# Maxima rows sent from ScalarE's queue, SyncE's order and VectorE's statistics rearranged in a ViT tower

## The chip, the cores and the metric

The kernel runs on one core of one Trainium2 chip. The metric is the time of one execution on the device in microseconds, as the median of several runs. Engines are named as the profile names them: PE is TensorE's matmuls and PEld its weight loads, DVE is VectorE, ACT ScalarE, POOL GpSimd, SP SyncE; SPq and ACTq are rows of DMA instructions issued by SP and ACT.

## What is computed

32 images of 3 x 256 x 256 pass an edge filter, one attention block and one feed-forward block. Cut to what matters:

```
gray = 0.2989*R + 0.587*G + 0.114*B
h    = (|scharr_x(gray)| + |scharr_y(gray)|) / 2        # 256 rows of 256 = 256 tokens
h    = concat([cls_tok, h], axis=1)                     # 257 tokens
# attention, 16 heads of 16, causal
q, k, v = split(layernorm(h) @ w_qkv + b_qkv)
h    = h + softmax(mask(q @ k.T / 4)) @ v @ w_out + b_out
# feed-forward with fake quantisation: one scale for the whole tensor
xq   = fake_quant(layernorm(h), clip_x)                 # scale from max |layernorm(h)| over all images
h    = h + fake_quant(silu(xq @ Wg.T) * (xq @ Wu.T), clip_down) @ Wd.T
```

The scale of the feed-forward input needs the maximum over all images, so the kernel has two parts: attention for all images, then the feed-forward block.

## The kernel before

**Pipeline.** The attention part is a software pipeline. `pipeline(eng, step)` runs `step(n, n % 2)` for n from 0 to B + LAST - 1 on every engine: steps 0 to 7 are written out, 8 to 29 are a hardware loop of two steps per round, 30 and up are written out again. In step n the engines work on several images at once: image n is loaded and turned gray, bW = n - 1 is saved to and gathered from DRAM, bC = n - 2 goes through the edge convolution and the first layernorm, bP = n - 3 through the projections to queries, keys and values, bS = n - 4 through the scores, bT = n - 5 through the rest of the transposed scores, the exponentials and the outputs, and bO = n - 6 through the division by the softmax sum, the output projection, the residual and the statistics of the second layernorm. The order within a step is written out by hand for each engine; semaphores do the rest, and a waiting instruction holds all that stands behind it on its engine.

**The two passes over the scores.** PE computes the scores of two heads at a time, `scores(u)` for u = 0..7 (L1005, mask added at L1008). DVE takes their row maxima, `maxima(bS, u)` (L788, L790). After u = 3 and u = 7 PE transposes the negated maxima of eight heads, `turn_max(half_)` (L1112), and DVE copies them into `mpart[half_]`, `split` (L805). A DMA puts them into rows SR and SR + 1 of `qst` (`max_rows`, L357), where they are two more rows of the contraction. So `scores_t(b, par, u)` (L1022), the scores transposed, come out with the maximum subtracted, and ACT takes their exponential (L580). `scores_t` waits for `m_loaded[0]` at u = 0 and for `m_loaded[1]` at u = 4. POOL masks the diagonal of two pairs of heads, `select(b, g)` (L463, L465), and `outputs(b, par, g)` (L1041) waits for that. In PE's order `scores_t(bS, par, 0)` stands ahead of `outputs(bT, odd, 3)`; in the next step `edges(0)` (L1060) waits for `msplit` of the second half, because both use the PSUM tile `M[1]`.

**SP, in order within a step.** The second half of the maxima of bT (`max_rows(bT, odd, 1)`); the moves of `yun` (L368, four DMAs) and `rec` (L372) for bO; gray planes of bW to DRAM (two DMAs); the next image (L304, three DMAs); the gathers of bW from DRAM (six DMAs, L393), behind waits for the gray planes saved and for the convolution of bC; the first half of the maxima of bS (`max_rows(bS, par, 0)`); the row of values of bS (L398); the keys (L404, six DMAs, waiting for the last `scores_t` of bT and `k_low`); the queries (L408, six DMAs, waiting for POOL's `q_low`); the softmax sums of bT (L412, `den`, four DMAs).

**ACT, in the middle of a step.** The exponential 7 of bT, the cast of `qpart` (L638), the exponential 0 of bS, the normalised rows `xhat` (L646), and so on; at the step's end the exponential 2 of bS and the scaling of image n by the gray weights (L660), then exponential 3 in the next step.

**DVE, around the block that is moved.** In step n: `split(bT, 1)`, `maxima(bS, 0)`, the reciprocal of `den` for bO (L862), `maxima(bS, 1)` to `(5)` with the edge work between them, the residual add of bO (L889), `maxima(bS, 6)`, `resid_stats(bO)` (L842 to L852), the values of bP, `maxima(bS, 7)`, then x2, its largest value and the mean for bO (L909 to L915). POOL's `pow` for bO (L507) lies between the two. At n = NW2 (36) DVE also prepares the weights of the down projection.

Of the kernel before, what the change touches and what calls it, by code (L numbers as in the profile page):

```python
# [10 lines left out]
P = 128  # L11
# [62 lines left out]
def vit_tower(nc, x, cls_tok, scharr, w_qkv, b_qkv, w_out, b_out, clip_x, clip_down,  # L74
# [8 lines left out]
    with ctx:  # L83
# [171 lines left out]
        LAST = 6  # L255
# [37 lines left out]
        NW0, NW2 = 3, B + LAST - 2  # L293
# [4 lines left out]
        def _(sp):  # L298
            xv = x.rearrange("b c (t p) w -> b p c t w", p=P)

            def load_x(b, par):
                src = xv[b] if isinstance(b, int) else xv[bass.ds(b, 1)].rearrange("o p c t w -> (o p) c t w")
                for c in range(CH):
                    sp.dma_start(xin[par][:, c, :, :], src[:, c]).then_inc(x_loaded[par], 16)  # L304
# [40 lines left out]
            def load_down():  # L345

                sp.wait_ge(gray_step, 2 * (B - 1))
# [5 lines left out]
            def max_rows(b, par, half_):  # L353

                if valid(b):
                    wait(sp, msplit, b, 2, half_ + 1)
                    sp.dma_start(qst[par][SR:SR + 2, 8 * half_:8 * half_ + 8, :], mpart[half_][:, :]  # L357
                                 ).then_inc(m_loaded[half_], 16)

            def step(n, par):  # L360
# [3 lines left out]
                max_rows(bT, odd, 1)  # L364
                if valid(bO):
# [6 lines left out]
                    sp.dma_start(rec[:, :], den[:, :]).then_inc(rec_moved, 16)  # L372
                if valid(bW):
                    wait(sp, gray_step, bW, 2, 2)
                    wait(sp, gst_loaded, bC - 1, 96, 96)
                    for t in range(QT):
                        sp.dma_start(gray_dram[odd][1 + P * t:1 + P * t + P, 1:1 + IMG],
                                     gray[:, t, :]).then_inc(gray_saved, 16)
# [5 lines left out]
                if valid(bW):  # L384
                    wait(sp, gray_saved, bW, 32, 32)
# [8 lines left out]
                max_rows(bS, par, 0)  # L394
# [23 lines left out]
                if isinstance(n, int) and n == B:  # L418
                    load_down()
# [4 lines left out]
        def _(pool):  # L424
# [43 lines left out]
            def step(n, par):  # L468
                bC, bP, bS, bT, bO = n - 2, n - 3, n - 4, n - 5, n - 6

                select(bT, 1)
                if valid(bS):
# [31 lines left out]
                if valid(bO):  # L504
                    wait(pool, ln2, bO, LN, LN)
                    wait(pool, x2_step, bO - 1, XS, XS)
                    nc.gpsimd.tensor_tensor(rstd2[:, rows2(bO)], ve2[:, :], half[:, :], ALU.pow  # L507
                                            ).then_inc(rs2_done, 1)
# [1231 lines left out]
```

## Time and profile before

| | |
|---|---|
| runs | 1157.46, 1163.3, 1168.16 us, median 1163.3 |
| the profiled execution | 1157.32 us, span 1155.6 us |
| mean granted clock of TensorE | 0.955 |
| busy share of the span | PE 86%, DVE 71%, ACT 59%, POOL 47% |

The span runs from the first to the last instruction of the one execution that was profiled. The attention part ends at about 936 us, the rest is the feed-forward block. Busy time does not count instructions that issue DMAs or handle semaphores. Times in the rows are microseconds from the start of the span.

### The profile page before, as it was taken

How to read it: one execution, taken by the hardware profiler on the slowest of the kernel's cores; microseconds unless marked ns; L12 is line 12 of the kernel's file. 1: busy time of each engine (PE TensorE's matmuls, PEld its weight loads, DVE VectorE, ACT ScalarE, POOL GpSimd, SP SyncE). 2: the span in 40 equal slices, each digit the busy share in tenths (PEclk: the TensorE clock that was granted, in tenths of full speed). 3: DMA queues.
4: the chain of work that ended last, by engine and by line, in shares of the span. 5: the costliest groups of instructions: out<-in, count | busy, mean ns of one | idle time of the engine just before them, and what ended most of it. 6: DMA issues, size and time to landing. Idle time of an engine off the chain costs nothing. (4 is left out here: it accounts for less than half of the span.)

```text
span 1155.6 us, 28368 instructions
## 1 busy us (share of the span) xinstructions
PE 989.1 (86%) x9742; PEld 709.7 (61%) x9742; DVE 814.8 (71%) x1969; ACT 686.6 (59%) x1171; POOL 538.1 (47%) x685
## 2 busy tenths in 40 slices
PE   6768989899999999899999998999888888887665
PEld 5446766666667676667676676676676643333454
DVE  4565566766677777766777777666666449998787
ACT  1345555666666566666666666665553237876776
POOL 5335455565555655565556555655443242220000
PEclk7888999999999999999999999999998989998989
DMA  7665555555556555555565555453422005501874
GB/s 200 149 138 145 132 136 143 133 128 134 133 154 151 137 148 148 129 130 138 152 152 135 149 148 130 130 139 100 116 63 63 12 1 200 200 1 50 265 227 151
DMA packets 156017, 152.93 MB, mean 132 GB/s; under 512 B 28175, under 2 KB 152372, under 8 KB 153908
## 3 DMA queue, kind: packets, MB, share of 16 engines
q1 hardware_dynamic: 154440, 152.14, 48.7%
q8 instruction: 35, 0.57, 0.2%
q10 hardware_dynamic: 1516, 0.01, 0.1%
q14 instruction: 26, 0.21, 0.1%
HBM read 67.49 MB, written 28.35 MB: 83 GB/s over the span
## 5 line engine op out<-in xcount | busy, mean ns | idle before, releaser
L580 ACT ACTIVATE prob<-ST 128x772 f32<-128x772 f32 x256 | 209.5, 818 | 152.4 <-PE ST L1022 147.7
L788 DVE TENSOR_REDUCE mneg<-SX 128x2 f32<-128x258 f32 x256 | 107.5, 420 | 224.7 <-PE SX L1008 224.5
L1005 PE MATMUL SX<-kst,qst 96*128 96x257 bf16 (+1 forms) x1024 | 160.4, 250 | 18.3 <-DMA qst<-qpart 7.6
L790 DVE TENSOR_REDUCE mneg<-SX 128x2 f32<-128x514 f32 x256 | 173.9, 679 | 0.0
L1022 PE MATMUL ST<-qst,kst 98*128 98x256 bf16 (+2 forms) x1536 | 138.0, 222 | 16.3 <-DMA qst<-mpart 15.9
L465 POOL TENSOR_SCALAR_AFFINE_SELECT prob<-prob 128x1016 f32<-128x1016 f32 x128 | 142.6, 1114 | 0.0
L1008 PE MATMUL SX<-mask_s,ident_b 128*128 128x256 bf16 x512 | 142.4, 278 | 0.0
L1022 PEld LDWEIGHTS ST<-qst,kst 98*128 98x128 bf16 x1536 | 120.3, 99 | 34.5 <-DMA qst<-mpart 14.7
L1005 PEld LDWEIGHTS SX<-kst,qst 96*128 96x128 bf16 x1024 | 91.9, 99 | 64.3 <-issue 28.4
L1041 PE MATMUL G<-prob,vaug 128*32 128x256 f32 (+2 forms) x3072 | 116.2, 280 | 11.9 <-POOL prob L465 10.6
L1041 PEld LDWEIGHTS G<-prob,vaug 128*32 128x32 f32 x3072 | 82.7, 111 | 44.6 <-POOL prob L465 16.0
L513 POOL TENSOR_TENSOR gray<-xin 128x512 f32<-128x512 f32 x32 | 40.6, 1269 | 93.9 <-ACT xin L660 93.8
L485 POOL TENSOR_TENSOR kpart<-kqr,kpart 128x512 bf16<-128x512 f32 x32 | 37.1, 1158 | 95.7 <-ACT kpart L632 95.7
L1060 PE MATMUL M<-gst,cw 102*32 102x256 f32 x1024 | 72.7, 401 | 9.0 <-DVE mpart L805 7.8
L1450 ACT ACTIVATE work<-GU,gsc 128x512 f32<-128x512 f32 x96 | 65.5, 686 | 23.6 <-PE GU L1658 23.3
L480 POOL TENSOR_TENSOR kqr<-kqr,kpart 128x512 f32<-128x512 f32 x32 | 37.0, 1157 | 88.9 <-ACT kqr L592 88.9
L463 POOL TENSOR_TENSOR tick<-half 128x2 f32<-128x2 f32 x128 | 30.1, 235 | 100.1 <-ACT prob L580 100.0
L1073 PE MATMUL M<-xT,wqkv 128*128 128x256 f32 x256 | 75.9, 421 | 0.0
L1711 PE MATMUL GU<-wdT,hq 128*128 128x256 bf16 x384 | 52.9, 304 | 25.8 <-ACT hq L1478 25.8
L1658 PE MATMUL GU<-work,wgT 128*128 128x512 bf16 x192 | 57.8, 383 | 18.1 <-ACT work L1436 11.0
L1084 PE MATMUL M<-xT,wqkv 128*128 128x256 f32 x256 | 72.3, 404 | 0.1
L1133 PE MATMUL M<-wop,yn 128*128 128x256 f32 x256 | 65.9, 402 | 0.8 <-DVE yn L870 0.8
(232 smaller groups left out, 2056.9 us busy)
## 6 DMA issues: line engine op xcount, KB each, us to landing
kst<-kpart SPq DMA_DIRECT2D x192, 128.5 KB, 2.5
xin<-in_x SPq DMA_DIRECT2D x96, 256.0 KB, 4.1
gst<-gray_dram SPq DMA_DIRECT2D x96, 256.0 KB
qst<-qpart SPq DMA_DIRECT2D x192, 128.0 KB, 2.4
h_dram<-hb SPq DMA_DIRECT2D x8, 1280.0 KB, 4.6
gray_dram<-gray SPq DMA_DIRECT2D x64, 128.0 KB, 3.0
result<-oy SPq DMA_DIRECT2D x32, 256.0 KB, 3.6
hb<-h_dram SPq DMA_DIRECT2D x5, 1280.0 KB, 6.6
```

Source lines behind the costliest of these rows:

```text
L465: nc.gpsimd.affine_select(p, p, [[0, 4], [-1, 2], [1, P - 1]], ALU.is_ge, 0.0, base=1, channel_multiplier=-1).then_inc(sel_done, 1)
L580: nc.scalar.activation(prob[:, g % 2, 2 * (u % 2):2 * (u % 2) + 2, 0:QEND], ST[:, :, 0:QEND], ACT.Exp).then_inc(exp_done, 1)
L788: nc.vector.tensor_reduce(mneg[:, 0, u // 4, 0, at], SX[:, :, S0:S0 + P + 1], AX.X, ALU.max, negate=True)
L790: nc.vector.tensor_reduce(mneg[:, 1, u // 4, 0, at], SX[:, :, S1:S1 + T], AX.X, ALU.max, negate=True).then_inc(max_done, 1)
L1005: mm(SX[:, r, at:at + k], qst[par][0:SR, 2 * u + r, P * t:P * t + P], kst[par][0:SR, 2 * u + r, 0:k], start=t == 1, stop=False)
L1008: last = mm(o, ident_b[:, :], mask_s[:, :, :], start=False, stop=True)
L1022: last = mm(ST[0:KEYS[k], r, QAT[k]:QAT[k] + QN[k]], kst[par_][:, i, KFIRST[k]:KFIRST[k] + KEYS[k]], qst[par_][:, i, Q0[k]:IMG], start=Tru ...
L1041: last = mm(o, vaug[par_][0:KEYS[k], k, head_at(4 * g + j), :], prob[0:KEYS[k], g % 2, j, QAT[k]:QAT[k] + QN[k]], start=k == 0, stop=k == ...
L1060: last = mm(M[1][32 * j:32 * j + 32, IMG * f:IMG * f + IMG], cw[:, f, :], gst[:, 4 * t + j, :], start=True, stop=True)
L1073: last = mm(M[m][:, 0:IMG], wqkv[:, c, D + P * m:D + P * m + P], xT[:, c, 1:T], start=c == 0, stop=c == KC - 1)
L1084: last = mm(M[0][:, 0:IMG], wqkv[:, c, P * m:P * m + P], xT[:, c, 1:T], start=c == 0, stop=c == KC - 1)
L1133: last = mm(M[0][:, D * t:D * t + D], yn[:, c, P * t:P * t + P], wop[:, c, :], start=c == 0, stop=c == KC - 1)
```

## The change

1. `LAST` goes from 6 to 7: one more step. A new index bR = n - 7 takes over the second layernorm: `resid_stats` comes one step later, between `maxima(bS, 0)` and `maxima(bS, 1)`, and the normalisation, its maximum and the mean between `maxima(bS, 1)` and `maxima(bS, 2)`. POOL's `pow` moves with it, to the place behind `select(bT, 1)`.
2. Both halves of the maxima are sent by ACT: `send_max(0)` behind the cast of `qpart` and ahead of exponential 0 of bS, `send_max(1)` behind the scaling of image n, at the step's end. SP's two `max_rows` are gone, so the value row and the keys follow the gathers directly.
3. The image is loaded by one DMA instead of three, the gray planes are saved by one instead of two, and the counts of `x_loaded` and `gray_saved` follow.
4. `load_down` moves from the end of step B to step B + 1 behind `rec`, and waits for `gray_step` of all images. NW2 and the step of the `sd_row` copy keep their numbers.

The constants, then SP:

```diff
-        LAST = 6
+        LAST = 7
-        NW0, NW2 = 3, B + LAST - 2
+        NW0, NW2 = 3, B + 4
...
-                for c in range(CH):
-                    sp.dma_start(xin[par][:, c, :, :], src[:, c]).then_inc(x_loaded[par], 16)
+                sp.dma_start(xin[par][:, :, :, :].rearrange("p c t w -> p (c t) w"), src).then_inc(x_loaded[par], 16)
-                sp.wait_ge(gray_step, 2 * (B - 1))
+                sp.wait_ge(gray_step, 2 * B)
-            def max_rows(b, par, half_):
-
-                if valid(b):
-                    wait(sp, msplit, b, 2, half_ + 1)
-                    sp.dma_start(qst[par][SR:SR + 2, 8 * half_:8 * half_ + 8, :], mpart[half_][:, :]
-                                 ).then_inc(m_loaded[half_], 16)
-                max_rows(bT, odd, 1)
+                if isinstance(n, int) and n == B + 1:
+                    load_down()
-                    for t in range(QT):
-                        sp.dma_start(gray_dram[odd][1 + P * t:1 + P * t + P, 1:1 + IMG],
-                                     gray[:, t, :]).then_inc(gray_saved, 16)
+                    sp.dma_start(gray_dram[odd][1:1 + IMG, 1:1 + IMG].rearrange("(t p) w -> p t w", p=P),
+                                 gray[:, :, :]).then_inc(gray_saved, 16)
-                max_rows(bS, par, 0)
-                if isinstance(n, int) and n == B:
-                    load_down()
```

POOL:

```diff
                 select(bT, 1)
+                if valid(bR):
+                    wait(pool, ln2, bR, LN, LN)
+                    wait(pool, x2_step, bR - 1, XS, XS)
+                    nc.gpsimd.tensor_tensor(rstd2[:, rows2(bR)], ve2[:, :], half[:, :], ALU.pow
+                                            ).then_inc(rs2_done, 1)
```

ACT:

```diff
+                def send_max(half_):
+                    if valid(bS):
+                        wait(act, msplit, bS, 2, half_ + 1)
+                        act.dma_start(qst[par][SR:SR + 2, 8 * half_:8 * half_ + 8, :], mpart[half_][:, :]
+                                      ).then_inc(m_loaded[half_], 16)
                     nc.scalar.copy(qpart[:, 1, :, :], qr[:, :, :]).then_inc(q_mid, 1)
+                send_max(0)
                 exponential(bS, 0)
                         nc.scalar.mul(xin[par][:, c, :, :], xin[par][:, c, :, :], GRAY[c]).then_inc(gray_scaled, 1)
+                send_max(1)
```

DVE:

```diff
+                resid_stats(bR)
                 maxima(bS, 1)
+                if valid(bR):
+                    wait(dve, rs2_done, bR, 1, 1)
+                    for t in range(QT):
+                        nc.vector.tensor_scalar(x2[:, t, :], h2[:, row_of(bR, t), :].rearrange("p o d -> p (o d)"),
+                                                ag2[:, t, 0:1], rstd2[:, row_of(bR, t)],
+                                                ALU.subtract, ALU.mult).then_inc(x2_step, 1)
+                    wait(dve, x2_step, bR, XS, 2)
+                    nc.vector.tensor_reduce(colmax[:, rows2(bR)], x2[:, :, :], AX.X, ALU.max,
+                                            apply_absolute_value=True)
+                    nc.vector.tensor_reduce(mean2[:, rows2(bR)], ag2[:, :, 0:1], AX.X, ALU.max).then_inc(x2_step, 2)
                 maxima(bS, 2)
                 maxima(bS, 6)
-                resid_stats(bO)
                 maxima(bS, 7)
-                if valid(bO):
-                    wait(dve, rs2_done, bO, 1, 1)
...
```

The lines removed at the end are the same as those added ahead of `maxima(bS, 2)`, with bO for bR.

## Rows read from the trace of the kernel before

**Rows 1.** Busy time by stretch: stretch, length, PE, PEld, DVE, ACT, POOL, clock, DMA share, GB/s
```profile
300.00:700.00 400.00, 366.30 (x4187) 277.33 (x4188) 290.18 (x750) 251.91 (x451) 236.46 (x298) 1.00 0.55 141
499.00:504.00 5.00, 5.00 (x69) 3.89 (x61) 3.34 (x11) 3.83 (x9) 1.78 (x2) 1.00 1.04 267
504.00:506.00 2.00, 1.87 (x13) 1.33 (x11) 2.00 (x4) 1.11 (x2) 1.80 (x3) 1.00 0.24 48
```

**Rows 2.** The `rec` transfer, one per step, 300 to 700: ns min/median/max, first and last start
```profile
L372 SPq DMA_DIRECT2D rec<-den x16: 577/577/578, 314.1 to 699.5; - x16
```

**Rows 3.** Waits of TensorE, 300 to 700: us in total, times, longest
```profile
PE M L1112 <- DVE mneg L797: 10.9, 16, 0.9
PE M L1060 <- DVE mpart L805: 6.0, 16, 0.6
PE G L1041 <- POOL prob L465: 5.8, 12, 0.8
PE ST L1022 <- DMA qst<-mpart: 5.4, 13, 0.8
```

**Rows 4.** Timeline, middle of a step: start, duration, engine, line [idle before, releaser]
```profile
503.21 0.69 SPq L357 DMA_DIRECT2D qst<-mpart  x1
...
504.57 0.62 ACT L638 CAST qpart<-qr 128x512 bf16<-128x512 f32 x1
504.81 3.81 SPq L404 DMA_DIRECT2D kst<-kpart  x6
...
506.52 1.12 POOL L465 TENSOR_SCALAR_AFFINE_SELECT prob<-prob 128x1016 f32<-128x1016 f32 x1
506.55 0.54 PE L1022 MATMUL ST<-qst,kst 98*128 98x256 bf16 x6 [0.27 <-DMA qst<-mpart]
...
507.69 0.90 PE L1041 MATMUL G<-prob,vaug 128*32 128x256 f32 x24 [0.61 <-POOL prob L465]
```

**Rows 5.** Timeline, from this step into the next
```profile
513.58 1.66 ACT L660 ACTIVATE xin<-xin 128x512 f32<-128x512 f32 x3
515.65 0.40 DVE L805 CAST mpart<-M 16x256 bf16<-16x256 f32 x1
516.08 0.69 SPq L357 DMA_DIRECT2D qst<-mpart  x1
516.20 1.07 PE L1060 MATMUL M<-gst,cw 102*32 102x256 f32 x16 [0.52 <-DVE mpart L805]
518.13 1.11 POOL L465 TENSOR_SCALAR_AFFINE_SELECT prob<-prob 128x1016 f32<-128x1016 f32 x1
518.93 0.43 DVE L788 TENSOR_REDUCE mneg<-SX 128x2 f32<-128x258 f32 x1 [1.69 <-PE SX L1008]
519.30 0.81 PEld L1041 LDWEIGHTS G<-prob,vaug 128*32 128x32 f32 x24 [0.16 <-POOL prob L465]
```

**Rows 6.** Timeline, steps 36 and 37, DVE and SP
```profile
912.32 0.69 DVE L889 TENSOR_TENSOR h<-h,M 128x512 f32<-128x512 f32 x1 [4.99 <-PE M L1133]
916.64 0.14 DVE L915 TENSOR_REDUCE mean<-ag 128x2 f32<-128x2 f32 x1
917.48 2.58 SPq L368 DMA_DIRECT2D yun<-yun  x4
922.37 0.35 DVE L862 RECIPROCAL den<-den 128x32 f32<-128x32 f32 x1
922.75 0.58 SPq L372 DMA_DIRECT2D rec<-den  x1
```

**Rows 7.** Timeline, a send of the maxima when little else is on the way
```profile
900.26 0.67 SPq L357 DMA_DIRECT2D qst<-mpart  x1
902.31 0.52 PE L1022 MATMUL ST<-qst,kst 98*128 98x256 bf16 x6 [0.30 <-DMA qst<-mpart]
```

**Rows 8.** Timeline, TensorE waiting for DMAs in the steps written out at the end
```profile
853.08 0.33 PE L1005 MATMUL SX<-kst,qst 96*128 96x257 bf16 x2 [0.78 <-DMA qst<-qpart]
860.37 1.13 PE L1121 MATMUL G<-rec,sel 16*128 16x256 f32 x4 [1.01 <-DMA rec<-den]
877.98 0.48 PE L1005 MATMUL SX<-kst,qst 96*128 96x257 bf16 x2 [1.78 <-DMA qst<-qpart]
```

More of the change, by code:

```diff
@@ L298, in _ @@
         def _(sp):
-            xv = x.rearrange("b c (t p) w -> b p c t w", p=P)
+            xv = x.rearrange("b c (t p) w -> b p (c t) w", p=P)
             def load_x(b, par):
-                src = xv[b] if isinstance(b, int) else xv[bass.ds(b, 1)].rearrange("o p c t w -> (o p) c t w")
-                for c in range(CH):
-                    sp.dma_start(xin[par][:, c, :, :], src[:, c]).then_inc(x_loaded[par], 16)
+                src = xv[b] if isinstance(b, int) else xv[bass.ds(b, 1)].rearrange("o p k w -> (o p) k w")
+                sp.dma_start(xin[par][:, :, :, :].rearrange("p c t w -> p (c t) w"), src).then_inc(x_loaded[par], 16)
             load_x(0, 0)
@@ L384, in step @@
                 if valid(bW):
-                    wait(sp, gray_saved, bW, 32, 32)
+                    wait(sp, gray_saved, bW, 16, 16)
                     wait(sp, conv_done, bC, 2, 2)
@@ L468, in step @@
             def step(n, par):
-                bC, bP, bS, bT, bO = n - 2, n - 3, n - 4, n - 5, n - 6
+                bC, bP, bS, bT, bR = n - 2, n - 3, n - 4, n - 5, n - 7
                 select(bT, 1)
+                if valid(bR):
[3 more added lines that the diff above has]
+                                            ).then_inc(rs2_done, 1)
                 if valid(bS):
@@ L503, in step @@
                 select(bS, 0)
-                if valid(bO):
[L505 to L508, printed above, removed]
                 if valid(n):
                     wait(pool, gray_scaled, n, 3, 3)
-                    wait(pool, gray_saved, n - 1, 32, 32)
+                    wait(pool, gray_saved, n - 1, 16, 16)
                     src = lambda c: xin[par][:, c, :, :]
@@ L657, in step @@
                 if valid(n):
-                    wait2(act, x_loaded, n, par, 48)
+                    wait2(act, x_loaded, n, par, 16)
                     for c in range(CH):
                         nc.scalar.mul(xin[par][:, c, :, :], xin[par][:, c, :, :], GRAY[c]).then_inc(gray_scaled, 1)
+                send_max(1)
                 if isinstance(n, int) and n == 3:
@@ L854, in step @@
             def step(n, par):
-                bC, bP, bS, bT, bO = n - 2, n - 3, n - 4, n - 5, n - 6
+                bC, bP, bS, bT, bO, bR = n - 2, n - 3, n - 4, n - 5, n - 6, n - 7
                 odd = 1 - par
@@ L905, in step @@
                 maxima(bS, 7)
-                if valid(bO):
-                    wait(dve, rs2_done, bO, 1, 1)
-                    for t in range(QT):
-                        nc.vector.tensor_scalar(x2[:, t, :], h2[:, row_of(bO, t), :].rearrange("p o d -> p (o d)"),
-                                                ag2[:, t, 0:1], rstd2[:, row_of(bO, t)],
-                                                ALU.subtract, ALU.mult).then_inc(x2_step, 1)
-                    wait(dve, x2_step, bO, XS, 2)
-                    nc.vector.tensor_reduce(colmax[:, rows2(bO)], x2[:, :, :], AX.X, ALU.max,
-                                            apply_absolute_value=True)
-                    nc.vector.tensor_reduce(mean2[:, rows2(bO)], ag2[:, :, 0:1], AX.X, ALU.max).then_inc(x2_step, 2)
                 if isinstance(n, int) and n == 3:
@@ L927, in step @@
                     go(nc.vector.tensor_scalar(sg[:, :], sg[:, :], 1 / QMAX, None, ALU.mult))
-                if isinstance(n, int) and n == B + LAST - 1:
+                if isinstance(n, int) and n == B + 5:
                     dve.wait_ge(w_pe, len(TW) + 1)
```

## The prediction

> **What bounds the kernel now.** I read the stretches first. From 300 to 700 us TensorE is busy for 366.30 of 400 us at a granted clock of 1.00, DVE for 290, ACT for 252 and POOL for 236 [rows 1]. So attention is a TensorE loop with about 8% of gaps, and only what closes or opens a gap counts. One image takes a step of 25.7 us: the `rec<-den` transfer, one per step, starts at 314.1 and for the 16th time at 699.5 [rows 2]. The waits of TensorE in the same stretch name the gaps [rows 3]: second-pass maxima transposed (L1112) wait on DVE for 10.9 us, the edge convolution (L1060) waits on `mpart` for 6.0, the outputs (L1041) on POOL's mask for 5.8, the transposed scores (L1022) on the DMA of the maxima for 5.4. Over 15.6 steps that is 1.8 us per step.
>
> These waits are not independent, and the timeline shows which of them ends last. Two places in a step are held by POOL.
>
> Place one, in the middle of a step [rows 4]. The first half of the maxima goes out on SP at 503.21 and releases L1022 at 506.55. But the next matmul group, the outputs L1041 at 507.69, starts as the mask (L465, 506.52 for 1.12) ends at 507.64. L1022 takes 0.54, so it may start as late as about 507.1 and nothing is lost: the DMA has 0.55 us of slack here.
>
> Place two, over the step boundary [rows 5]. ACT scales the new image (L660, until 515.24), POOL adds the planes (L513 and L515), then masks (L465, 518.13 to 519.24), and the outputs L1041 load their weights at 519.30 after 0.16 us of waiting for POOL. In this stretch TensorE has waited for `mpart` (0.52 us at L1060) and for DVE (at L1112), and then meets a mask that ends in the same tenth of a microsecond.
>
> **The change, part by part.**
>
> *DVE block moved.* `resid_stats` and the normalisation with its maxima (L842 to L915; in the tail they take DVE from 913.01 to 916.78, or 3.8 us with a wait for POOL in it [rows 6]) leave the places around `maxima(6)` and `maxima(7)` and go, one step later, between `maxima(0)`, `(1)` and `(2)`. There DVE idles 1.69 us before L788 at 518.93 [rows 5], and the timeline shows a wait of this kind before the next one too, so I cost the block at nothing there. If the cover is gone (L852 or L909 held up while POOL masks), `maxima(2)` comes at most one mask (1.11 us) late, and `scores(3)`, which needs it, stands behind three other matmul groups: still covered. Where it left, the seventh maxima start 0.2 us earlier and `mpart` (L805, 515.65) 1.0 us earlier. TensorE gains that, an estimated 0.2 at L1112 and on average 0.4 at L1060 (6.0 us over 16 waits [rows 3]), and loses it again at L1041, because the chain ACT, gray planes, mask is unchanged and ends at 519.24. Worth per step: below 0.1 where POOL holds, 0.3 to 0.6 where it does not. TensorE's row counts only 12 waits for the mask in 16 steps [rows 3], so at place two POOL is last by little and not in every step. I take nothing for the loop here and keep -0.6 as the far end.
>
> *POOL's power (L507) moved.* 0.69 us from ahead of the gray planes to behind `select(bT, 1)`. In the old place POOL then waited for ACT anyway; in the new one it waits more than 2 us for the keys of the next image. Nothing.
>
> *Maxima sent by ACT.* SP loses two issues of 0.69 us per step, ACT gains them [rows 4, 5]. ACT is busy 63% of the time [rows 1]. The second half goes out behind L660, which ends at 515.24, with `mpart` ready by then: that is 0.8 us earlier than the 516.08 of SP. The exponential behind it can start when the issue is over, at 515.9, and the mask that needs it starts only at 518.13. Nothing lost. The first half is the delicate one. On ACT it stands behind L638, which starts at 504.57 and takes 0.62, so it is issued between 504.6 and 505.2 instead of at 503.21: 1.4 to 2.0 us later [rows 4].
>
> What does it take to land? Before, 503.21 to 506.55, or 3.3 us. A send with empty DMA engines took 900.26 to 902.31, or 2.05 us [rows 7]. The difference has a cause in the trace: from 499 to 504 the DMA share is 1.04, the engines are full of the image load and the gathers that SP issued ahead of the send, and it falls to 0.24 from 504 to 506 [rows 1]. From ACT at 504.6 to 505.2 the send meets nearly empty engines and the first keys. With 2.05 us it lands at 506.6 to 507.25; the limit is 507.1. So the cost is 0 to 0.15 us per step, and with 3.34 us it would be (504.6 or 505.2) + 3.34 + 0.54 + 0.05 = 508.5 or 509.1 against 507.69, which is 0.8 to 1.4. I take 0.1, near the quiet end, since the traffic that made the 3.3 is over. Times 28 steps with an image load in flight: +3 us.
>
> The Trainium skill, page "DMA: Bandwidth & Descriptors", section "Issuing engines are not separate DMA queues", says that issuing from another engine saves only the sequencer's time, since all transfers run on the same DMA engines. By that rule a later issue would simply land later. Its section "Queues, rings and completion order" says that a DMA engine takes turns, packet by packet, between the queue of SP and that of ACT, which would let the send pass the gathers. No row of this trace has both queues loaded in the loop. The first rival below has the mechanism of the first rule, with its times from rows.
>
> *SP's order.* Without the first send, the value row goes out right behind the gathers and the keys start when the last transposed scores are done, about 503.6 instead of 504.81 [rows 4]. The queries still wait for POOL's `q_low` in the loop, so there nothing is gained. In the unrolled steps at the end the queries go out later and `scores(0)` waits for them 0.78 us at 853.08 and 1.78 at 877.98 [rows 8]. The keys 1.0 us earlier give 0.8 and 1.0. The missing second send lets the moves of `yun` and then `rec` go 0.7 us earlier, the length of its issue; TensorE waits for `rec` 1.01 us at 860.37 [rows 8] and in the two steps after it, so 3 x 0.7 = 2.1. With `load_down` no longer ahead of the second send, I estimate 0.7 in its step. Sum 4.6 us.
>
> *One DMA instead of three and two.* Image load and gray planes save about 1.4 us of SP time and start the image load earlier; the gathers wait for the convolution either way. Nothing, except that it thins the traffic ahead of the maxima.
>
> *Tail.* After the add of image 30 (L889, ends 913.01) DVE does the block until 916.78, then the weights of the down projection, and only at 922.37 the reciprocal of image 31, for which `rec` goes out at 922.75 [rows 6]. In the new order the block is not there. The reciprocal could come 3.7 us earlier, but `rec` also stands behind the four moves of `yun`, which end at 917.48 + 2.58 = 920.06: the gain is 922.75 - 920.1 = 2.6 us. The block of image 30 then fills the time until the spread of `rec` is back. One more step (37 becomes 38) holds only the block of image 31, which was last before too: 0.
>
> *Head.* The first eight steps are unrolled as the last are, and SP's order is the same; I give them a little under half of the 4.6, an estimate: -2 us.
>
> Sum: +3 - 4.6 - 2.6 - 2 = -6.2, and -0.8 for the few steps in which POOL does not hold: -7.0. The profiled execution took 1157.3 us (span 1155.6), so 1150.3 on its terms. It stands 6 us below the median of the three runs, 1163.3, and lies within their spread. On the median: **1156 us**.
>
> **Rivals.**
> *The send lands as late after its issue as before (slower).* Place: L1022 behind `exponential(bT, 7)` and L638. Price 0.8 to 1.4 us per step as worked out above, 1.1 x 28 = +31, less the 9 of gains at both ends: 1185. It decides from the point where the landing passes 507.1 by more than 0.3 us. For it: the keys now start at 503.6, ahead of the send, and crowd it as the gathers did. Against: the DMA share of 0.24 from 504 to 506 [rows 1]. Chance 0.18.
> *A wash.* The keys cost the send some 0.25 us more than I take: 0.35 x 28 = +10 against -9, 1163. Chance 0.22.
> *POOL does not hold the boundary (faster).* Then both DVE waits pay, 0.6 x 28 = -17, and with -9 the time is 1137. For it: L1041 waits on POOL in only a part of the steps. Against: the mask's end at 519.24 and the outputs at 519.30 [rows 5]. Chance 0.12.
> *My forecast*, own range 1149 to 1161: 0.48.
>
> **How the numbers follow.** A measurement of this kernel can tell about 1% from no change, so faster means below 1151.7 and slower above 1174.9. Faster: 0.12 plus the lower quarter of my own case, 0.25. Slower: the first rival, nearly whole, 0.17. Same: 0.58. The range must reach toward both ends: 1143 to 1180 leaves out most of the 0.12 and part of the 0.18.
>
> **What the profile after would show.** Right, if TensorE waits for `mpart` at L1060 are gone and those for POOL at L1041 have grown by about as much; if L1022 waits on the maxima not much longer than before; if the step stays at 25.7 to 25.8 us; if the last `rec<-den` comes some 2.6 us sooner after the add of image 30. Wrong toward slow, if L1022 in the middle of a step waits 1 us or more for `qst<-mpart` and the mask before it has long ended. Wrong toward fast, if the step falls to 25.2. The DVE block would be the mistake if `maxima(2)` starts late and `scores(3)` waits for it.

## The result and the profile after

The changed kernel is slower: 1191.4 us (median of four, 1178.5 to 1196.8) against 1160.4 us in runs beside it (1155.0 to 1168.2). The ratio is 1.023, with a 95% interval of 1.017 to 1.029. One of these four executions (1196.8 us) and one of the ten of e4 below (3365 us) were in a slower state: they count in the medians and not in the ratios. The forecast was 1156 us in a range of 1143 to 1180, so it missed on the slow side.

| | before | after |
|---|---|---|
| median, us | 1160.4 | 1191.4 |
| profiled span, us | 1155.6 | 1189.2 |
| first to last `rec` transfer (31 steps), us | 795.5 | 829.7 |
| from the last `rec` transfer to the end, us | 232.8 | 230.7 |

The second half of the table says where to look. The transfer of `rec` is the clock of the pipeline, one per image. The row of this tile, of the kernel before and then of the kernel after (duration in ns as least, median and most, then first and last start):

```profile
L372 SPq DMA_DIRECT2D rec<-den x32: 577/577/590, 127.3 to 922.8; - x32
```

```profile
L363 SPq DMA_DIRECT2D rec<-den x32: 577/583/1282, 128.8 to 958.5; - x32
```

The 31 steps take 34.2 us more, and that is the whole difference of the spans (33.6). The head costs 1.5 more, what follows the last transfer 2.1 less. So the loss is in the steps of attention and has to be explained from one step. Waits of TensorE in the kernel after, 300 to 700 us (total in us, times, longest), the view of [rows 3]:

```profile
PE ST L1019 <- DMA qst<-mpart: 25.6, 15, 2.1
PE G L1038 <- POOL prob L454: 7.7, 14, 0.8
PE M L1109 <- DVE mneg L794: 7.7, 14, 0.6
```

Four things stand in it. The transposed scores (L1019, before L1022) wait 25.6 us for the DMA of the maxima where they waited 5.4: 1.7 us each time. The wait of the edge convolution for `mpart`, 6.0 us in [rows 3], is gone, as forecast. The wait for POOL's mask has risen from 5.8 to 7.7, as forecast in direction. The wait at the maxima transposed fell from 10.9 to 7.7.

The timeline shows the long wait, in the middle of a step (start, duration, engine, line, and in brackets the idle time and its releaser). It is the place of [rows 4]:

```profile
524.05 3.96 SPq L395 DMA_DIRECT2D kst<-kpart  x6
...
525.01 0.62 ACT L633 CAST qpart<-qr 128x512 bf16<-128x512 f32 x1
525.10 0.63 ACTq L605 DMA_DIRECT2D qst<-mpart  x1
...
526.72 1.11 POOL L454 TENSOR_SCALAR_AFFINE_SELECT prob<-prob 128x1016 f32<-128x1016 f32 x1
...
528.69 0.54 PE L1019 MATMUL ST<-qst,kst 98*128 98x256 bf16 x6 [1.97 <-DMA qst<-mpart]
...
529.16 1.57 PE L1038 MATMUL G<-prob,vaug 128*32 128x256 f32 x24
```

SP begins to issue the keys at 524.05. ACT issues the maxima at 525.10, and TensorE is released at 528.69, 3.6 us later. The mask ended at 527.83, long before, so the cover that [rows 4] showed (0.55 us of slack under the mask) is used up and the rest is loss. The last line shows something else: the 24 matmuls of the outputs take 1.57 us, where they took 0.90 in [rows 4].

That is TensorE's clock. The steps come in two lengths, 26.3 to 27.2 and 27.9 to 28.1 us, seven of each among the 14 that start between 300 and 700 us. By stretch, the columns of [rows 1], first the 300 to 700 us, then a short step and the long one behind it:

```profile
300.00:700.00 400.00, 354.66 (x3909) 267.45 (x3911) 275.37 (x697) 235.76 (x424) 217.66 (x277) 0.97 0.53 134
462.51:488.65 26.14, 23.37 (x271) 17.80 (x268) 19.10 (x49) 16.13 (x30) 14.95 (x19) 1.00 0.54 139
488.65:516.76 28.11, 25.19 (x272) 18.97 (x269) 18.80 (x49) 16.23 (x30) 14.98 (x19) 0.94 0.55 138
```

Both steps hold the same work (271 and 272 matmuls). One takes 26.14 us at a granted clock of 1.00 (2.4 GHz), the other 28.11 at 0.94, a mean over parts at 2.4 and, as the row at 502 us below shows, parts at 1.2 GHz. In the long one TensorE waited longer at L1019 and then ran slowly for a while:

```profile
476.01 1.97 PE L1092 MATMUL M<-wqkv,xT 128*128 128x256 f32 x8
...
500.22 0.54 PE L1019 MATMUL ST<-qst,kst 98*128 98x256 bf16 x6 [1.60 <-DMA qst<-mpart]
...
503.11 3.00 PE L1092 MATMUL M<-wqkv,xT 128*128 128x256 f32 x8
```

```profile
502.00:504.00 2.00, 2.00 (x12) 1.67 (x10) 1.03 (x2) 1.86 (x4) 0.00 (x0) 0.50 0.73 196
```

After the wait of 1.60 us the clock is at 0.50 (1.2 GHz) from 502 to 504, and eight matmuls of L1092 take 3.00 us. In the short step the same eight take 1.97.

### The profile page after: what moved, and what is told of

It is laid out like the page before. It is cut to its first block and busy times, and to the rows that moved or that the text cites. A ratio compares the mean times of both kernels' runs of the same rounds, so it can differ in the third digit from the quotient of the medians.

```text
span 1189.2 us, 28206 instructions
## 1 busy us (share of the span) xinstructions
PE 1002.7 (84%) x9731; PEld 721.4 (61%) x9742; DVE 820.8 (69%) x1969; ACT 686.9 (58%) x1171; POOL 535.3 (45%) x685
## 5 line engine op out<-in xcount | busy, mean ns | idle before, releaser
L1019 PE MATMUL ST<-qst,kst 98*128 98x256 bf16 (+2 forms) x1536 | 142.9, 226 | 53.8 <-DMA qst<-mpart 53.8
L1002 PE MATMUL SX<-kst,qst 96*128 96x257 bf16 (+1 forms) x1024 | 165.2, 255 | 13.3 <-DVE mneg L787 5.5
L1019 PEld LDWEIGHTS ST<-qst,kst 98*128 98x128 bf16 x1536 | 123.9, 101 | 74.2 <-DMA qst<-mpart 43.6
L1005 PE MATMUL SX<-mask_s,ident_b 128*128 128x256 bf16 x512 | 146.1, 285 | 0.0
L1038 PE MATMUL G<-prob,vaug 128*32 128x256 f32 (+2 forms) x3072 | 122.1, 290 | 18.9 <-POOL prob L454 18.9
L1038 PEld LDWEIGHTS G<-prob,vaug 128*32 128x32 f32 x3072 | 86.2, 114 | 53.8 <-POOL prob L454 23.2
L1092 PE MATMUL M<-wqkv,xT 128*128 128x256 f32 x256 | 73.5, 437 | 0.0
L1070 PE MATMUL M<-xT,wqkv 128*128 128x256 f32 x256 | 72.7, 406 | 0.0
L1081 PE MATMUL M<-xT,wqkv 128*128 128x256 f32 x256 | 72.5, 405 | 0.1
L1708 PE MATMUL GU<-wdT,hq 128*128 128x256 bf16 x384 | 52.6, 302 | 23.6 <-ACT hq L1475 23.6
L1655 PE MATMUL GU<-work,wgT 128*128 128x512 bf16 (+1 forms) x185 | 57.0, 387 | 17.9 <-ACT work L1433 8.8
L579 ACT ACTIVATE kpart<-M,bqk 128x256 bf16<-128x256 f32 x64 | 30.5, 477 | 63.7 <-PE M L1070 63.7
```

What stands on the lines that cost most here:

```text
L1002: mm(SX[:, r, at:at + k], qst[par][0:SR, 2 * u + r, P * t:P * t + P], kst[par][0:SR, 2 * u + r, 0:k], start=t == 1, stop=False)
L1005: last = mm(o, ident_b[:, :], mask_s[:, :, :], start=False, stop=True)
L1019: last = mm(ST[0:KEYS[k], r, QAT[k]:QAT[k] + QN[k]], kst[par_][:, i, KFIRST[k]:KFIRST[k] + KEYS[k]], qst[par_][:, i, Q0[k]:IMG], start=Tru ...
L1038: last = mm(o, vaug[par_][0:KEYS[k], k, head_at(4 * g + j), :], prob[0:KEYS[k], g % 2, j, QAT[k]:QAT[k] + QN[k]], start=k == 0, stop=k == ...
L1070: last = mm(M[m][:, 0:IMG], wqkv[:, c, D + P * m:D + P * m + P], xT[:, c, 1:T], start=c == 0, stop=c == KC - 1)
L1081: last = mm(M[0][:, 0:IMG], wqkv[:, c, P * m:P * m + P], xT[:, c, 1:T], start=c == 0, stop=c == KC - 1)
```

## The experiments

The first question was whether the loss comes from the late landing of the first half (theory A in the quoted texts) or from the other edits. After that came the clock after the wait (theory C), the keys issued ahead of the send (theory P), and the size of what the moved DVE block gives (theory M). Each quoted text gives its own numbers. All ratios are to the kernel before, run on the same chip. Steps of the loop are read as the distance of two `rec` transfers. Where a kernel has other line numbers, the tiles tell which wait is meant: `ST<-qst,kst` with `qst<-mpart` are the transposed scores, `SX` with `qst<-qpart` the scores waiting for the queries, `G` with `prob` the outputs.

### e1: the first half back on SP

On the kernel after; SP sends it ahead of the value row, as before:

```diff
+                max_rows(bS, par, 0)
                 if valid(bS):
                     wait(sp, v_last, bS, 1, 1)
...
-                send_max(0)
                 exponential(bS, 0)
```

> The changed kernel with one edit taken back: the first half of the maxima is sent by SP again, behind the gathers and ahead of the value row and the keys; the second half stays on ACT. Theory A (the whole loss is the first half's send landing late): L1022's waits on the maxima fall from 25.6 us in 300 to 700 to about 5, the step returns to 25.6 or 25.7 us, and the time is 1148 to 1155 us, below the kernel before by what I forecast for the steps at both ends. Theory B (the block moved on DVE and POOL, or the second half on ACT, costs something of its own in the loop): the step stays above 26 us and the time above 1170.

Measured: 1150.1 us, ratio 0.990 (0.987 to 0.993). The loop's step is 25.53 us. Waits of TensorE in this kernel, 300 to 700:

```profile
PE G L1045 <- POOL prob L462: 12.2, 30, 0.6
PE M L1116 <- DVE mneg L801: 8.8, 16, 0.6
PE ST L1026 <- DMA qst<-mpart: 3.4, 12, 0.6
PE SX L1009 <- DMA qst<-qpart: 3.2, 11, 0.4
```

One send of 8 KB, moved from ACT to SP, takes 41 us off, 1191.4 to 1150.1. It is the whole loss and more: the rest of the change makes the kernel 1% faster. The first-half send takes 3.25 us to land here, about what it took before (3.34, [rows 4]), but it is issued early enough.

### e2: the same send on ACT, one exponential earlier

```diff
+                send_max(0)
                 exponential(bT, 7)
...
-                send_max(0)
                 exponential(bS, 0)
```

> The changed kernel with send_max(0) moved on ACT from behind the cast of qpart to ahead of exponential 7, where mpart has just become ready: issued about when SP issued it before, ahead of the keys, still on ACT's queue. Theory A1 (the send was late because it was issued late, behind the start of the keys): it lands 2.1 to 3.3 us after its issue, L1022 waits no more than 0.5 us, step 25.7, time 1148 to 1158. Theory A2 (ACT's queue is served badly while SP's is loaded, whatever the order): 3.5 us or more from issue to landing again, and more where the gathers are still under way; L1022 waits 0.3 to 0.8 us, step 25.7 to 26.2, time 1155 to 1170.

Measured: 1154.8 us, ratio 0.993 (0.990 to 0.996). A step of it, and its waits:

```profile
504.11 0.62 ACTq L605 DMA_DIRECT2D qst<-mpart  x1
...
504.49 3.83 SPq L395 DMA_DIRECT2D kst<-kpart  x6
...
508.40 0.54 PE L1019 MATMUL ST<-qst,kst 98*128 98x256 bf16 x6 [1.24 <-DMA qst<-mpart]
```

```profile
PE ST L1019 <- DMA qst<-mpart: 15.1, 16, 1.4
```

The send now leaves ahead of the keys but close behind the gathers, and lands 4.3 us after its issue in this step (median 4.0 of the 15 between 300 and 700 us). SP's own send, in e1, takes 3.3 at that place. So ACT's queue did not carry the 8 KB past the gathers: that it is another queue gave it no precedence. What makes the difference of 0.7 us is open, since more than the queue differs: in e2 the value row goes out ahead of the send and the keys start 0.38 us after its issue, in e1 both come behind it and the keys start 1.6 us after. The waits are 0.9 us each rather than 1.7, and no step of the loop shows a clock under 1.00. The kernel is 37 us faster than after for 0.8 us less of waiting in each of the 22 steps of the loop, or 18 us. That is the first hint that the loss has two parts. The landing and the waits are those of theory A2 or worse, while the time is within theory A1's range.

### e3: no keys ahead of the send

SP holds the keys until ACT has reached the cast after which it sends:

```diff
                     wait(sp, k_low, bP, 1, 1)
+                    wait(sp, q_mid, bP, 1, 1)
```

> The changed kernel with one wait added: SP issues the keys only when the cast of qpart (q_mid) is done, so the send of the first half on ACT goes out ahead of the first key DMA, at its unchanged place in ACT's order. Theory A1a (the keys crowd the send): issue to landing falls from 3.5 us to 2.1 to 2.5 us, L1022 waits at most 0.5 us, and the time is 1150 to 1162. Theory A1b (the tail of the gathers holds it, the keys are innocent): issue to landing stays at 3.3 to 3.5, L1022 waits 1.2 us or more, the time stays at 1180 to 1195.

Measured: 1162.0 us, ratio 1.001 (0.998 to 1.004).

```profile
512.63 0.62 ACTq L606 DMA_DIRECT2D qst<-mpart  x1
513.25 3.83 SPq L396 DMA_DIRECT2D kst<-kpart  x6
...
514.81 0.54 PE L1020 MATMUL ST<-qst,kst 98*128 98x256 bf16 x6 [0.56 <-DMA qst<-mpart]
```

With no keys ahead, the send from ACT releases TensorE 2.18 us after its issue in this step, and lands in a median of 2.06. That is the 2.05 of the lone send of [rows 7], with which the forecast had reckoned. The wait is 0.56 instead of 1.97, and the loop's step falls to 25.53 us. Yet the kernel stays 12 us behind e1, which has the same step. The delayed keys push the queries back, and between 300 and 700 us the scores now wait 8.9 us for them (3.2 in e1):

```profile
PE SX L1003 <- DMA qst<-qpart: 8.9, 15, 0.7
...
PE ST L1020 <- DMA qst<-mpart: 7.6, 16, 0.9
```

That does not lengthen the loop: its 22 steps take 569.9 us in e3 and 571.1 in e1. As far as the profiled executions show it (1161.0 us against 1154.5 of span), the loss is in the steps written out at both ends. In the first ones the scores wait for the queries too, up to 2.1 us at a time, but they do so in e1 as well, so that late queries are what costs e3 the time is not shown.

### e10: one key ahead instead of two

The same wait, set behind the first of the six key transfers (128 KB each):

```diff
                         sp.dma_start(kst[odd][s:SR:NS, :, :], kpart[:, i, :, :]).then_inc(kst_loaded[odd], 16)
+                        if s == 0:
+                            wait(sp, q_mid, bP, 1, 1)
```

> The changed kernel, with SP's wait for the cast of qpart put behind the first of the six key DMAs instead of ahead of it, so that one key DMA is issued ahead of the send of the first half and five behind. With none ahead the wait at L1022 was 0.5 us per step and the time 1162; with about two ahead (the changed kernel) 1.7 and 1191. Theory P (the send is served after what was issued ahead of it, in proportion): L1022 waits 0.9 to 1.1 us, no step above 27 in the loop, time 1163 to 1170. Theory Q (a single key DMA ahead is enough for the full delay): waits 1.5 us or more, 1180 or more.

Measured: 1152.6 us, ratio 0.993 (0.989 to 0.997).

```profile
504.48 4.75 SPq L395 DMA_DIRECT2D kst<-kpart  x6
505.55 0.62 ACTq L607 DMA_DIRECT2D qst<-mpart  x1
...
508.18 0.54 PE L1021 MATMUL ST<-qst,kst 98*128 98x256 bf16 x6 [1.01 <-DMA qst<-mpart]
```

```profile
PE ST L1021 <- DMA qst<-mpart: 13.3, 16, 1.3
```

Together with e3 and the kernel after this is a series in which only the number of key transfers ahead of the send changes:

| keys ahead | median landing of the send, us | mean wait at the transposed scores, us | time, us |
|---|---|---|---|
| none (e3) | 2.06 | 7.6 / 16 = 0.5 | 1162.0 |
| one (e10) | 2.42 | 13.3 / 16 = 0.8 | 1152.6 |
| two (after) | 3.39 | 25.6 / 15 = 1.7 | 1191.4 |

The landings and the waits follow the keys, so the cause of the late landing is shown. The times do not follow in that order. With two ahead the clock falls. With none ahead the loop is as fast as with one (569.9 and 569.1 us for its 22 steps), and the steps written out at both ends are slower. In the last 170 us or so before the last `rec` the scores wait 8.9 us for the queries in e3 and 3.4 in e10. That fits late queries as the reason, but e1 waits 7.9 there and is no slower than e10. One key ahead gives steps of 25.5 to 26.2 us at full clock. The time itself was below the 1163 to 1170 us expected, which had been reckoned up from e3's 1162.

### e4: is part of the loss the clock?

On the kernel after, matmuls on constants are put in front of the wait for the first half, into a PSUM tile that is written afresh afterwards. They take 1.90 us a step and change nothing that is computed:

```diff
+                        if u == 0:
+                            keep_warm(4, ST)
                         if u % 4 == 0:
                             wait(pe, m_loaded[u // 4], b, 16, 16)
```

> The changed kernel with four matmuls on constants (fp32, 256 columns, about 0.4 us each) put ahead of TensorE's wait for the first half of the maxima; they write a PSUM bank whose content is not used and fill 1.6 us of a wait of 1.3 to 2.1. The output is unchanged. Steps of the changed kernel come in two lengths, 26.2 us after a wait of 1.3 and 28.1 after one of 1.6 to 2.1. Theory C (the longer ones are the clock that falls to half after the stall): all steps become 26.2 to 26.4, the granted clock in the loop returns to 1.00, and the time falls by about 15 x 1.9 = 28 us to 1160 to 1167. Theory D (the longer steps are longer because the send lands later, the clock is a side effect): the steps of 28 stay and the time stays above 1180.

Measured: 1163.1 us, ratio 1.002 (0.999 to 1.004). The constant matmuls of one step, the stretch of 300 to 700 and the `rec` transfers in it:

```profile
509.64 1.90 PE L940 MATMUL ST<-one 128*128 128x256 f32 x8
```

```profile
300.00:700.00 400.00, 378.15 (x4174) 289.99 (x4167) 284.73 (x722) 243.46 (x439) 224.28 (x285) 1.00 0.54 137
```

```profile
L363 SPq DMA_DIRECT2D rec<-den x15: 583/584/584, 310.1 to 681.5; - x15
```

The clock is 1.00 through the stretch, no step there is above 26.9 us, and the mean step is 371.4 / 14 = 26.5, where the kernel after has 27.3 and e1 25.5. The send still lands late, in a median of 3.2 us. So theory C holds in the loop: of the 1.8 us that the late send costs in a step, 0.8 come back when the wait is filled with matmuls that nobody needs, and about 1.0 stays as the length of the stall (the filler of 1.90 us is itself longer than some of the waits).

The busy time says the same in another way. The row of 300 to 700 us in e1:

```profile
300.00:700.00 400.00, 369.44 (x4212) 278.94 (x4208) 294.75 (x749) 253.67 (x456) 232.88 (x296) 1.00 0.56 143
```

Divided by the steps in it, TensorE is busy 24.2 us and idle 3.1 in a step of the kernel after, and busy 23.6 and idle 1.9 in one of e1. By this estimate 1.1 us of the difference is idle time and 0.6 is the same work at a lower clock.

The whole kernel got 28 us faster (1191.4 to 1163.1), the number that theory C had named, but for a different sum. In the profiled executions the 22 steps of the loop give 16.0 of 30.8 us. The rest is in the steps written out at both ends and behind them, where the constant matmuls run too: from 125 to 300 us the clock is 1.00 in e4, 0.96 in the kernel after and 0.94 in e1. So e4 also repairs what the late send had not caused, and the 28 us are not the clock's share of the 41.

### e5 and e6: the other edits

e5 is the kernel before with nothing but both sends moved to ACT:

```diff
-                max_rows(bT, odd, 1)
...
-                max_rows(bS, par, 0)
...
+                send_max(0)
                 exponential(bS, 0)
...
+                send_max(1)
```

> The kernel before with only the two sends moved to ACT, at the places of the changed kernel; the block on DVE and POOL, the DMA counts, LAST and load_down stay as they were. Theory A (the first half on ACT behind the start of the keys is the whole loss): L1022 waits 1.3 to 2.1 us per step as in the changed kernel, and the time is 1190 to 1200, at or above the changed kernel's 1191. Theory B' (the moved block or the merged DMAs are a good part of the loss): the time is 1165 to 1180.

Measured: 1208.3 us, ratio 1.040 (1.033 to 1.047), above what was expected.

```profile
PE ST L1028 <- DMA qst<-mpart: 22.9, 15, 2.2
PE M L1118 <- DVE mneg L803: 12.3, 14, 1.0
PE M L1066 <- DVE mpart L811: 5.6, 14, 0.6
PE G L1047 <- POOL prob L463: 0.8, 4, 0.2
```

The sends alone cost 49 us. The wait for `mpart` at the edges (5.6) is there again, and the mask never binds (0.8): with the DVE block in its old place, and the sends on ACT, DVE is last at the boundary and not POOL. The rest of the change is worth 17 us on top of it (1208.3 to 1191.4). One more wait is in the trace, of ACT for `mpart`:

```profile
  ACT prob L578: 29.4, 14
```

ACT reaches the second send before DVE has the rows ready. It issues it 1.2 us after the end of the scaling (median of 14), and exponential 3 stands behind it. In the kernel after it is issued 0.1 us before that end. How much of the 17 us this is was not tested.

e6 is the kernel after with both sends back on SP at their old places:

```diff
+                max_rows(bT, odd, 1)
...
+                max_rows(bS, par, 0)
...
-                send_max(0)
...
-                send_max(1)
```

> The changed kernel with both sends back on SP at their old places: only the block on DVE and POOL, the extra step, the merged DMAs and load_down are left of the change. My forecast for these parts was nothing in the loop and a gain at the tail: 2.6 us from the block, 0.7 from load_down. So 1154 to 1158 against about 1161 before. If the second half on ACT is what makes the step 25.53 instead of 25.65 us in the run with the first half on SP, the step here is 25.65 again; if the moved block does that, it is 25.53.

Measured: 1148.2 us, ratio 0.988 (0.982 to 0.995), below the 1154 to 1158 expected.

```profile
PE G L1045 <- POOL prob L463: 11.6, 29, 0.7
PE M L1116 <- DVE mneg L801: 8.8, 16, 0.6
PE ST L1026 <- DMA qst<-mpart: 4.9, 13, 0.7
PE SX L1009 <- DMA qst<-qpart: 2.7, 8, 0.4
```

```profile
L371 SPq DMA_DIRECT2D rec<-den x17: 577/582/583, 289.7 to 698.3; - x17
```

The step is 408.6 / 16 = 25.54 us against 25.7 before [rows 2]. In the waits stands what the forecast had described: that for `mpart` at the edges has gone and the mask's has doubled, 11.6 us against 5.8 [rows 3]. e6 and e1 differ by the second half alone, and neither step (25.54 and 25.53) nor time (1148.2 and 1150.1) tells them apart: the second half may sit on either queue.

### e7 and e9: which of the other edits is it?

e7 is e1 with the image load in three transfers and the gray planes in two, as before:

```diff
-                sp.dma_start(xin[par][:, :, :, :].rearrange("p c t w -> p (c t) w"), src).then_inc(x_loaded[par], 16)
+                for c in range(CH):
+                    sp.dma_start(xin[par][:, c, :, :], src[:, c]).then_inc(x_loaded[par], 16)
...
-                    sp.dma_start(gray_dram[odd][1:1 + IMG, 1:1 + IMG].rearrange("(t p) w -> p t w", p=P),
-                                 gray[:, :, :]).then_inc(gray_saved, 16)
+                    for t in range(QT):
+                        sp.dma_start(gray_dram[odd][1 + P * t:1 + P * t + P, 1:1 + IMG],
+                                     gray[:, t, :]).then_inc(gray_saved, 16)
```

> The run with the first half on SP (1150 us), with the image load again in three DMAs and the gray planes in two. I forecast nothing for the merging. If right, 1148 to 1153. If the later image load thickens the traffic ahead of the first half, its landing goes from 3.25 us after the issue to 3.4 or more, L1022 waits 0.2 us longer per step, and the time is 1154 to 1158.

Measured: 1150.9 us, ratio 0.989 (0.983 to 0.996), against 1150.1 for e1. Merging the transfers is worth nothing that can be measured.

e9 is the kernel before with the DVE block, POOL's power and `LAST` alone changed; sends, transfers and `load_down` are those of before:

```diff
+                resid_stats(bR)
                 maxima(bS, 1)
+                if valid(bR):
+                    wait(dve, rs2_done, bR, 1, 1)
...
                 maxima(bS, 6)
-                resid_stats(bO)
```

> The kernel before with only the second layernorm moved on DVE and POOL (and the extra step); both sends on SP, DMA counts and load_down as before. The run with both sends on SP took 1148.2 us, 12 below the kernel before, where I had forecast 3 for these parts. Theory M (the moved block is what gains: 0.1 us per step in the loop, more where the mask does not hold TensorE, and the tail): 1147 to 1151. Theory N (load_down and the merged DMAs give a good part): 1153 to 1157.

Measured: 1149.3 us, ratio 0.989 (0.981 to 0.998). The block alone gives the gain of e1 and e6, within what these runs resolve. The `rec` transfers of the whole kernel:

```profile
L372 SPq DMA_DIRECT2D rec<-den x32: 577/577/589, 128.7 to 921.0; - x32
```

The 31 steps take 792.3 us against 795.5, and from the last transfer to the end (span 1149.8) it is 228.8 against 232.8. The head takes 1.4 more. So the profiled executions show 5.8 of the 12 us between the medians, 3.2 in the steps and 4.0 behind them. The profiled execution of the kernel before (1157.3 us) is 4.2 us under the median of the runs beside e9 (1161.5), and that of e9 (1151.6) is 2.2 over its own. That is the remainder, so the size of the gain is known only to a few us.

### e8 and e11: warm ends

In e1 the first five steps after the first `rec` still take 26 to 31 us, with waits for the queries of up to 2.1 us in the stretch from 100 to 240 and a clock of 0.91 to 0.96. Three constant matmuls in front of the scores of the steps written out, on e1 (e8) and on e6 (e11):

```diff
                             wait(pe, max_done, bS - 1, 8, 8)
+                            if ends:
+                                keep_warm(3, SX)
```

> The run with the first half on SP (1150 us), with three matmuls on constants ahead of TensorE's wait for keys and queries in scores(0), in the steps that are written out (up to 7 and from 30). There scores(0) waits 1.5 to 2.2 us for the queries, and the granted clock falls behind it: these steps take 28 to 30 us against 25.5 in the loop. The three matmuls fill 1.2 us of each wait. If the clock is what makes these steps long, they become 26 to 27 us and the time falls to 1136 to 1143. If it is the DMAs behind them, nothing changes or it is up to 3 us slower.

> The run with both sends on SP (1148.2 us) with three matmuls on constants ahead of the wait of scores(0) in the steps written out. Its steps there take 26.3 to 27.9 us against 25.5 in the loop. If the clock is part of that, 1143 to 1147; if the matmuls only take the time of the wait and more, 1148 to 1150.

Measured: e8 1147.4 us, ratio 0.990 (0.986 to 0.994); e11 1149.8 us, ratio 0.989 (0.981 to 0.996). Against e1 and e6 that is 2.7 us less and 1.6 us more, within the scatter of either. The gain expected, to 1136 to 1143 and to 1143 to 1147 us, did not come. The clock did rise: the first three steps after the first `rec` run at 1.00 in e8 (0.94, 0.91 and 0.92 in e1) and take 80.5 us instead of 87.5. But the same three steps take 81.0 us in e7, which has no constant matmuls in them and differs from e1 only in the split transfers. The first steps thus differ between profiled executions of nearly equal kernels by as much as was to be gained, and why is open.

## Why the prediction was wrong

**The failed step** is the landing of the first half: "With 2.05 us it lands at 506.6 to 507.25". The time of issue was right. ACT issues the send with the cast that stands ahead of it (525.10, the cast from 525.01), at the early end of the window in the forecast. The price of a send that meets nothing was right as well (2.06 us in e3). Wrong was the ground for using it: "the traffic that made the 3.3 is over". The DMA share of 0.24 from 504 to 506 in [rows 1] belonged to the order of before, in which the keys started at 504.81. The same forecast moved the keys to 503.6, ahead of the send, and took that as a gain for the queries, but it did not redraw the DMA traffic of the 2 us that it had itself refilled; "the first keys" are named there and given no price. In the kernel after, these 2 us look like this:

```profile
524.00:526.00 2.00, 1.87 (x11) 1.31 (x10) 2.00 (x4) 1.56 (x3) 1.80 (x3) 1.00 0.62 132
```

The DMA share is 0.62 where the forecast had read 0.24. Two key transfers stood ahead of the send and it landed in 3.39 us, past the 0.55 us of slack. The series of e3, e10 and the kernel after shows that nothing else was needed. The first rival had this mechanism ("the keys now start at 503.6, ahead of the send, and crowd it as the gathers did") and a price of 0.8 to 1.4 us a step, and was given 0.18. Its 1185 us is 6 below the measured median.

The Trainium skill, page "DMA: Bandwidth & Descriptors", says in section "Issuing engines are not separate DMA queues" that transfers issued by different engines run on the same 16 DMA engines and interleave. The runs agree: ACT's send took 3.39 us with two of SP's keys ahead and 2.06 with none. The Trainium skill says in the same page's section "Queues, rings and completion order" that a DMA engine takes turns between the queues, a packet at a time. The forecast read from this that the send could pass the gathers. e2 does not show that, since ACT's send took 4.0 us where SP's took 3.3.

**The term that was missing** is the clock. The forecast priced a stall at its length. A stall of 1.6 to 2.1 us in a loop in which TensorE had been 92% busy [rows 1] was followed by a stretch below the full clock and a step of 28.1 instead of 26.1 us. By e4 this is 0.8 of the 1.8 us that a step of the loop lost against e1; the stall's own length is the other 1.0. The first rival came out close by chance: it had no clock in it and a stall of 1.1 us for all 28 steps, and it reckoned with 9 us of gains. The Trainium skill, page "TensorE: Matmul & The Clock Gate", section "Part 1: The HAM clock gate", says that the throttled state is the default and that activity releases it. The trace agrees in kind: the long step shown above, with a wait of 1.60 us, is the one at 0.94, and the short one, with a wait of 1.26, is at 1.00.

**DVE block in the loop: right in mechanism, too small in size.** The forecast said that the wait for `mpart` at the edges would go and that the mask's would take its place, and took nothing for it but -0.8 in sum. That is what e6 shows, and its step of 25.54 against 25.7 gives some -3 us over the 22 steps of the loop. The medians give the block about -12 (e9). The third rival (POOL does not hold the boundary, step 25.2) is ruled out for the sends on SP. With the sends on ACT it may have been partly true: e5 has a mask wait of 0.8 us and lies 17 us above the kernel after, though ACT's wait for `mpart` is in that difference too.

The block raised no new wait of TensorE: in its new place its parts lie in DVE's idle time, as forecast. DVE itself now waits for POOL's power, 0.4 us in this step and 8.6 in 14 steps between 300 and 700 us, where the kernel before had no such wait.

```profile
514.70 1.01 DVE L865 TENSOR_SCALAR x<-h,ag,rstd 128x256 f32 x2 [0.43 <-POOL rstd L464]
```

**Tail: right.** In the kernel after, the last add and the last transfer of `rec`, the places of [rows 6]:

```profile
950.20 0.69 DVE L897 TENSOR_TENSOR h<-h,M 128x512 f32<-128x512 f32 x1 [4.99 <-PE M L1130]
...
955.36 3.04 SPq L359 DMA_DIRECT2D yun<-yun  x4
...
956.47 0.35 DVE L859 RECIPROCAL den<-den 128x32 f32<-128x32 f32 x1
...
958.50 0.58 SPq L363 DMA_DIRECT2D rec<-den  x1
```

From the add to the transfer it is 8.30 us, before 922.75 - 912.32 = 10.43: 2.1 sooner for a forecast of 2.6. The transfer stands directly behind the moves of `yun`, which is the limit the forecast had named.

**SP's order at the ends: half right, and given back.** From 834 to 970 the scores of the kernel after wait 1.0 us for queries; in the same stretch of before, 800 to 936, it is 3.5. That is 2.5 for a forecast of 1.8. The 2.1 for `rec` did not come (4.5 us against 4.7). And the maxima take back what was gained:

```profile
PE ST L1019 <- DMA qst<-mpart: 5.1, 3, 3.1
PE G L1118 <- DMA rec<-den: 4.5, 5, 1.5
...
PE SX L1002 <- DMA qst<-qpart: 1.0, 2, 0.6
```

**Head: wrong in sign.** I had transferred a gain to it by analogy, -2 us. From 100 to 240 us the transposed scores wait 9.1 us for the maxima (4.9 before), up to 2.6 at a time.

**One transfer instead of three and two: nothing**, as forecast (e7). **POOL's power and the second half on ACT: nothing**, as forecast (e6 against e1).

**The sum afterwards**: the block gives about -12 us (e9, interval 0.981 to 0.998 of the time before), the sends on ACT about +43 (e6 to after). The clock's share of these 43 is measured in the loop alone, an estimated 0.8 x 22 = 18 us. Together +31, as measured. The forecast had -7, with the block at -3.4 for tail and loop and the send at +3.

## What to carry to other kernels

When an edit moves a transfer later and another one earlier, draw the traffic of the new order before pricing the landing. A quiet stretch of the old trace is no evidence once something has been moved into it, and a small latency-bound send belongs ahead of bulk transfers, whichever engine issues it. A stall in a loop that keeps TensorE over 90% busy is priced twice, its own length and the slower clock behind it; here they were 1.0 and 0.8 us of each step. And when a filler is put into the whole kernel, read its effect stretch by stretch, since it can also repair what the change had not broken.

## What the runs showed of the hardware

An 8 KB send landed 2.06 us after its issue with nothing ahead of it, 2.42 with one 128 KB transfer issued ahead on another engine's queue, 3.39 with two, and 4.0 behind the gathers. Being on a queue of its own did not protect it. Whether it is held up where descriptors are made or at the DMA engines is open, and so is why ACT's send behind the gathers took 0.7 us more than SP's at that place.

In the kernel after, ACT issued the first send at most 0.09 us after the start of the cast ahead of it (525.01 and 525.10) and not at its end, so the place behind a 0.62 us cast cost less than it seems. The second send went out 0.5 us after the start of the last scaling ahead of it, 0.1 us before its end.

Several versions beat both kernels by about 1% (e6 1148.2, e8 1147.4, e9 1149.3, e1 1150.1 us). The runs don't tell them apart.
